# Decay factors in five buffers, made after each step's other ScalarE work; B broadcast first in the sixth step

## Time and profile before

| | us |
|---|---|
| median of 3 runs | 428.7 (428.37 to 428.83) |
| the profiled execution | 431.48 |
| its span, first to last instruction | 429.7 |
| PE busy | 340.4 (79%) |
| PEld busy | 205.5 (48%) |
| DVE busy | 252.1 (59%) |
| ACT busy | 209.9 (49%) |
| POOL busy | 248.5 (58%) |

### The profile page before, as it was taken

One profiled execution on the slowest core, in us unless ns is written; L12 is line 12 of the kernel. 1 busy time (PEld: TensorE's weight loads), 2 busy tenths in 40 slices (PEclk: granted clock), 3 DMA queues, 4 the chain that ended last, 5 costly groups with the idle time before them and its releaser, 6 DMA issues.

```text
span 429.7 us, 5678 instructions
## 1 busy us (share of the span) xinstructions
PE 340.4 (79%) x1780; PEld 205.5 (48%) x1780; DVE 252.1 (59%) x439; ACT 209.9 (49%) x488; POOL 248.5 (58%) x232
## 2 busy tenths in 40 slices
PE   8794868856778677875869586899999999999651
PEld 4352435623446244653435242466666666666441
DVE  2989797974958879688977676112122222222134
ACT  4678786737877678767964100322222222212103
POOL 2075999999978996789888302233233333331214
PEclk9986596965989769896986888999999999999967
DMA  7050110162114510242106950111111111111162
GB/s 209 8 101 3 38 35 31 47 219 50 50 50 82 188 50 26 65 148 84 51 24 218 374 193 0 49 41 46 37 51 49 50 49 37 50 37 38 37 195 99
DMA packets 29455, 34.46 MB, mean 80 GB/s; under 512 B 4074, under 2 KB 23826, under 8 KB 29426
## 3 DMA queue, kind: packets, MB, share of 16 engines
q1 hardware_dynamic: 24770, 26.36, 20.3%
q0 software_dynamic: 2208, 6.03, 4.6%
q10 hardware_dynamic: 2448, 1.71, 1.4%
HBM read 28.92 MB, written 5.18 MB: 79 GB/s over the span
## 4 chain that ended last, share of the span: by engine, by line
PE 36%; DVE 6%; DMA 2%; ACT 2%; POOL 2%; issue 2%; DVEq 0%; POOLq 0%; ACTq 0%
PE psS L1600 18%; PE psD L1619 5%; PE psO L1619 4%; PE psD L1610 2%; PE psS L1450 2%; PE psT L1595 1%; DMA c_rows<-z_out 1%; DVE experts L981 1%; POOL rstd L493 1%; DVE u_sb L1131 1%; PE psT L1379 1%; DMA delta<-x_rows,row_in 1%; DMA z_out<-delta,row_out 1%; PE psT L1444 0%; POOL rstd L492 0%
## 5 line engine op out<-in xcount | busy, mean ns | idle before, releaser
L1600 PE MATMUL psS<-experts,delta 128*128 x184 | 86.5, 593 | 0.5 <-ACT delta L818 0.5
L504 POOL TENSOR_TENSOR experts<-experts,c_rows 128x1024 f32<-128x1024 f32 x31 | 73.0, 2355 | 17.8 <-DVE experts L981 17.4
L981 DVE TENSOR_TENSOR_SCAN experts<-experts,psD 128x512 f32<-128x512 f32 x64 | 74.4, 1204 | 0.0
L572 POOL DMA_INDIRECT z_out<-delta,row_out x23 | 22.8, 991 | 88.4 <-ACT delta L832 88.4
L1379 PE MATMUL psT<-ident,probs_at 128*128 128x128 f32 x192 | 39.2, 340 | 23.4 <-ACT probT L727 23.4
L1205 DVE COPY u_sb<-psD 128x512 f32<-128x512 f32 x23 | 15.9, 692 | 68.7 <-PE psD L1610 68.7
L689 ACT ACTIVATE experts<-delta,A_sb 128x255 f32<-128x255 f32 x128 | 54.7, 517 | 0.5 <-DVE du L929 0.5
L972 DVE TENSOR_TENSOR psD<-du,psD 128x512 f32<-128x512 f32 x64 | 41.6, 688 | 13.2 <-PE psD L1337 12.9
L1600 PEld LDWEIGHTS psS<-experts,delta 128*128 128x128 f32 x184 | 33.1, 190 | 24.3 <-issue 23.3
L1379 PEld LDWEIGHTS psT<-ident,probs_at 128*128 128x128 f32 x192 | 27.4, 172 | 35.1 <-ACT probT L727 33.4
L507 POOL TENSOR_TENSOR experts<-experts 128x512 f32<-128x512 f32 x31 | 40.7, 1312 | 2.4
(11 more groups left out here) (236 smaller groups left out, 591.6 us busy)
## 6 DMA issues: line engine op xcount, KB each, us to landing
c_rows<-c_dram SPq DMA_DIRECT2D x32, 256.0 KB, 3.4
experts<-in_L_ffn_w_gate_dram SPq DMA_DIRECT2D x8, 512.0 KB, 5.9
experts<-in_L_ffn_w_up_dram SPq DMA_DIRECT2D x8, 512.0 KB, 6.9
experts<-in_L_ffn_w_down_dram SPq DMA_DIRECT2D x8, 512.0 KB, 8.1
x_in<-in_x_dram SPq DMA_DIRECT2D x4, 256.0 KB, 5.3
x_rows<-x_sb SPq DMA_DIRECT2D x4, 256.0 KB, 2.5
probs_at<-z_out SPq DMA_DIRECT2D x4, 256.0 KB, 5.1
c_rows<-z_out ACTq DMA_DIRECT2D x4, 256.0 KB, 6.3
```

What stands on the lines that cost most here:

```text
L504: pool.tensor_tensor(states[:, g % ST], states[:, g % ST], c_rows[:, g % CR].rearrange("p n (o s) -> p n o s", o=1).broadcast_to([P, 2, HA ...
L981: dve.tensor_tensor_scan(states[:, g % ST, n].rearrange("p h s -> p (h s)"), dA[:, g % DA, n].rearrange("p h s -> p (h s)"), psD[:, n, :], ...
L1600: ins = pe.matmul(psS[:, bank, :], xgT[:, s % 2, k, :], gate_up_of(bass.ds(e, 1), i)[:, k, :], start=(k == 0), stop=(k == FC - 1))
```

## The change

`dA` gets five places instead of three. Three stay where they were, two are a tile of their own (`dA_more`), and the helper `dA(i)` gives the place. GpSimd therefore zeroes five first columns at the start instead of three. A decay now waits for the scan five steps back instead of three.

In ScalarE's list the decays move. After step 0's work come decay(1), skip(0) and decay(2) as before, and after step 1's work of batch 0 decay(3). All others stand at the end of a step, behind its other work, by the table `DECAYS_AHEAD`: after m = 2 the decay of step 4, after m = 3 of step 5, after m = 4 of steps 6 and 7, after m = 5 of steps 8 and 9 (the next batch's first two), after m = 6 of step 10, after m = 7 of step 11. The end of step m is the same position as the start of step m + 1. The number of decays ahead of each step's other work is therefore, in a middle batch, for m = 0 to 7: before 1, 1, 1, 1, 1, 1, 1, 1; after 1, 0, 0, 1, 1, 2, 2, 1.

In TensorE's list of step m = 5 the two broadcasts of B for step 6 go, in the batches 0 to 2, from between the two halves of q to the place ahead of the transposes of x2.

```diff
-    DA, ST, CR, PR = 3, 5, 4, 8
+    DA, ST, CR, PR = 5, 5, 4, 8
+    SHARED = 3
+    DECAYS_AHEAD = ((), (), (4,), (5,), (6, 7), (8, 9), (10,), (11,))
...
+        dA_more = sb("dA_more", [P, DA - SHARED, 2, HALVES, S])
...
-        dA, at = carve(area, 0, DA, 2, HALVES, S)
+        dA_shared, at = carve(area, 0, SHARED, 2, HALVES, S)
...
+        def dA(i):
+            return dA_shared[:, i] if i < SHARED else dA_more[:, i - SHARED]
...
                 for m in range(NP):
                     g = NP * b + m
-                    if 0 < g < STEPS - 2:
-                        if (g + 2) % NP == 0:
-                            act.wait_ge(du_rdy, (g + 2) // NP + 1)
-                        decay(g + 2)
...
                         skip(0)
                         decay(2)
+                    elif g == 1:
+                        decay(3)
...
                     elif m == 7 and b + 1 < B:
                         take_k(b + 1)
                         take_v(b + 1)
+                    for ahead in DECAYS_AHEAD[m]:
+                        if NP * b + ahead < STEPS:
+                            if ahead == NP:
+                                act.wait_ge(du_rdy, b + 2)
+                            decay(NP * b + ahead)
...
                     elif m == 5:
-                        if not more:
-                            broadcast_b(g + 1, 0)
-                            broadcast_b(g + 1, 1)
+                        broadcast_b(g + 1, 0)
+                        broadcast_b(g + 1, 1)
                         if f >= 0:
                             transpose_x2(f)
...
                         if more:
                             project_qk(b + 1, 0, 0, psS[:, 1, :], q_ps)
-                            broadcast_b(g + 1, 0)
-                            broadcast_b(g + 1, 1)
                         if more:
                             project_qk(b + 1, 0, 1, psS[:, 1, :], q_ps)
```

More of the change, by code:

```diff
@@ L455, in _ @@
             for i in range(DA):
-                pool.memset(dA[:, i, :, :, 0:1].rearrange("p n h s -> p (n h) s"), 0.0).then_inc(zeroed, 1)
+                pool.memset(dA(i)[:, :, :, 0:1].rearrange("p n h s -> p (n h) s"), 0.0).then_inc(zeroed, 1)
             link(pool.memset(v_sb[:, :, :, HD:].rearrange("p q h d -> p (q h) d"), 0.0))
@@ L688, in decay @@
                     for half in range(HALVES):
-                        act.activation(dA[:, g % DA, n, half, 1:], delta[:, b, half, 1:], ACT.Exp,
+                        act.activation(dA(g % DA)[:, n, half, 1:], delta[:, b, half, 1:], ACT.Exp,
                                        scale=A_sb[:, half, 2 * m + n:2 * m + n + 1]).then_inc(dA_rdy, 1)
@@ L981, in scan @@
                     dve.tensor_tensor_scan(
-                        states[:, g % ST, n].rearrange("p h s -> p (h s)"), dA[:, g % DA, n].rearrange("p h s -> p (h s)"),
+                        states[:, g % ST, n].rearrange("p h s -> p (h s)"), dA(g % DA)[:, n].rearrange("p h s -> p (h s)"),
                         psD[:, n, :], 0.0, ALU.mult, ALU.add).then_inc(scanned, 1)
```

## The result

The changed kernel took **439.0 us** (median, 438.8 to 441.0) against 428.8 before: ratio 1.0245, 95% interval 1.0208 to 1.0281. Forecast were 430.9 us and a range to 433.3: the direction was right, the size was almost five times too small (+2.2 us forecast, +10.3 measured).

What follows compares the result with a forecast made beforehand. GpSimd was taken to bound the steps until 96 us, then a ring of TensorE, VectorE and ScalarE. Terms -1.6 + 1.9 + 1.9 = +2.2 us on 428.7 gave 430.9 us, own range 429.3 to 432.1, 8-in-10 range 427.4 to 433.3.

Steps and rivals of the forecast that it cites:

- Moved decays, batches 1 and 2: Ends of batches 1 and 2: two decays ahead of take_x2T and take_oT make the residual late, +1.9 us each.
- project_out waits for it: [...] and takes 1.89: Batch 1's end: project_out waits for take_oT, starts at 136.95 instead of 134.46, takes 1.89 us, ends at 138.84.
- route link: Batch 1: take_x2T starts at 131.42 instead of 129.82, so route starts at 132.05 instead of 130.70.
- hold on scan 6: Batch 1: scan 6 waits for decay(6), starting about 129.2 instead of 130.16, a gain of 0.95 us.
- rival (b): TensorE's clock falls at a batch's end, project_out 3.2 us: +1.3 in one batch, 432.2; two, 433.5; chance 0.16.
- About +1.9, covered: Batch 0's end: take_oT late, +2.6 less 0.6 gained in step 1, about +1.9, covered by GpSimd's backlog.
- The cover: GpSimd's backlog keeps its deviation at 95.82; batch 1's transposes move from 95.43 to about 97.3, short of ScalarE's 97.51.
- the 0.6 us gained early: Batch 0's second step: with decay(3) moved behind its work, the copy starts at 44.72 instead of 45.40.
- -1.6 us, if the transposes stay earlier than that: Batch 1's second step: without its decay, ScalarE's probabilities copy starts at 97.51, not 99.10, if transposes finish before 97.51.
- rival (a): TensorE's clock rises earlier in second steps: -1.8, 429.1 in one batch (chance 0.12); -3.6, 427.3 in both (0.09).
- 0, at most 0.1: Batch 3's end: only decays 6 and 7 stand ahead of take_x2T, whose reader stands behind six filler matmuls; cost 0.
- rival (d): GpSimd is the bound throughout and nothing moves: 428.7 us, chance 0.06.

## Why the prediction was wrong, point by point

1. **Moved decays, batches 1 and 2: mechanism right, a term mis-sized.** The step "project_out waits for it: [...] and takes 1.89" failed. It took 3.78. Scan 6 to residual grew from 6.9 to 11.4 us where 9.7 was forecast; the 1.7 between are project_out's clock. With fillers in the waits the steps 5 to 7 are 2.0 us longer than before in batch 1, 2.4 in batch 2: the forecast's 1.9. The route link (1.6 us late) and the hold on scan 6 are as forecast; scan 6 came 0.4 us sooner behind scan 5 in batch 1, not 0.95.
2. **The fall of the clock was rival (b), at 0.16, with a price of 1.3 a batch.** It came in all four batches; the ends of the batches 0, 1 and 2 take 1.8, 2.2 and 1.5 us less in the run with fillers. The price was too low because it was scaled from four transposes, 0.63 to 1.06 us, a ratio of 1.7, while the eight matmuls take twice as long, 1.89 to 3.78. The chance rested on one wait of 1.04 us before the change, after which the clock held. In the middle batches the clock fell behind the new wait before route, and before project_out's own. The runs with such a wait show both levels, so a single wait was no safe ground in either direction.
3. **Batch 0: cost wrong, cover right.** "About +1.9, covered" failed. Batch 1's first scan comes 4.8 us later, counted from batch 0's: project_out was slow, 3.68 us after a wait of 3.47, and the 0.6 us gained early was gone (point 6). The cover was sized rightly, 97.51 less 95.43, or 2.1 us. So 2.7 us of the 4.8 came through, where nothing was forecast to.
4. **The removed decay in batch 1: its condition failed.** "-1.6 us, if the transposes stay earlier than that": they came 2.17 us after ScalarE was ready, because batch 0's end was late, and a decay would have fitted in that wait. What was quicker in batch 1's start is the cover used up and 1.8 us of rival (a)'s clock. That clock was luck, since a run with the same program up to there shows the low level. Where batch 0's end isn't late, in the runs with later decays, the term is there, 1.2 us of the 1.6. The removed decays of the second steps of the batches 2 and 3 gave nothing, as forecast: from the batch's first scan to the copy it is 10.6 us before and after. Those of the third steps were not measured alone. The places gave nothing.
5. **Batch 3: "0, at most 0.1" failed.** The fillers there ran at the high clock, 1.46 us for six where the profile of before has 2.77, so route waited 1.71 us for take_x2T, and project_out fell to 3.57 us. That is 2.1 us. The fillers are at the high clock in the run with five places and the orders of before too; against that run the end is 4.2 us longer. The 1.2 us in batch 3's first steps go with the low clock of its second step, which that run shows too.
6. **The 0.6 us of batch 0's first steps** came and was gone by step 4, before it could count. Why is not shown.

In sum: -1.6 + 1.9 + 1.9 was forecast, +2.2; from the first scan to batch 3's residual +10.1 was measured. The 7.9 between are 2.7 of batch 0 and the removed decay (points 3 and 4), 2.3, 2.0 and 2.1 at the ends of the batches 1 to 3, and -1.7, -0.7 and +1.2 in the first steps of the batches 1 (behind that copy) to 3, in 1 and 3 with the clock of the second step. With fillers the loss falls from 10.3 to 4.2 us: about 6 us are the clock's, the rest is the order. What tips the clock one way or the other after the same wait stays open.

By the Trainium skill ("TensorE: Matmul & The Clock Gate", section "HAM oscillation — how this bites in real kernels") a wait between bursts of matmuls can throttle TensorE again, so that the next burst starts slow. The traces agree on what the next burst pays, 1.89 against 3.78 us for the same eight. The waits of that section are for a DMA and longer than those of the middle batches here, after which the clock fell in some and held in others. By the Trainium skill ("Perfetto Trace Analysis", section "Identifying the Most-Contended Engine") the most-contended engine is optimised first. The prediction drew rival (d) from it, no change; moving the work of ScalarE, the least busy of the four compute engines after 96 us, cost 2.4%, which speaks against that reading here.

## What to carry to other kernels

Making something ahead of time isn't free when its maker also hands over results: ask of each slot not when the work is needed but what stands behind it in that engine's list, and put it where the engine waits anyway (here ahead of the first exponentials, 3 us idle) rather than ahead of a copy that another engine is waiting for. When a late copy opens waits on TensorE, price the matmuls behind them at the low clock too, from rows of matmuls at both levels; here that case came in six of eight. When a gain hangs on a condition ("if the transposes stay earlier"), take the condition into the sum. And move one thing at a time: B first alone gains 3.2 us, the decays alone cost about 7 in three executions of four, and together they cost 10.3.

## What was not expected of the hardware

The granted clock fell after waits of 1.2 to 1.6 us, and not each time: in one profiled execution the same wait before route was followed by 1.00 in batch 1 and 0.50 in batch 2 (fillers before project_out only). Matmuls of one form took 379 ns in the median before the change and 634 after it. A filler burst of 1.5 us in the first wait kept the high level; in one batch a burst in the second wait ran at the low level (1.87 us for four) and the clock was back when project_out ran. Executions of one kernel differ along with the mean granted clock: 429.4 us at 0.897 to 436.5 at 0.880 with one decay less ahead of take_oT, 429.1 at 0.902 to 437.1 at 0.884 with the decays alone.
